# A fused attention and feed-forward layer: residual added by DMA, part of the layer norm and token mix on ACT, new orders of work

## The reference, cut to what matters

```
xn  = layernorm(x)
out = x + attn(xn) + ffn(xn)

attn: q, k, v = silu(short_conv(xn @ Wq)), ...k, ...v ;  beta = sigmoid(xn @ Wb)
      delta   = chunked delta rule(l2norm(q), l2norm(k), v, beta), chunks of 32, a state S carried along L
      ms      = (three depthwise convolutions of v with 3, 15, 31 taps) @ kernel_mix_w @ channel_mixer_w
      hdn     = gelu([xn, mean|ms|, mean|delta|, mean|v|] @ fusion_w1 + b1)
      w       = softmax((hdn @ fusion_w2 + b2) per head over 3)
      o       = rmsnorm(w0 * ms + w1 * delta + w2 * v) * o_norm_w ;  result o @ Wo
ffn:  xp      = xn shifted by one token
      xr      = mu_r * xn + (1 - mu_r) * xp ;  xk = mu_k * xn + (1 - mu_k) * xp
      result  = sigmoid(xr @ W_r.T) * (relu(xk @ W_k.T)^2 @ W_v.T)
```

## Time and profile before

| | |
|---|---|
| median of 3 runs | 3716.8 us (3714.63 to 3717.57) |
| the profiled execution | 3716.15 us |
| its span, first to last instruction | 3714.3 us |
| PE busy | 3491.5 us, 94% |
| DVE busy | 3536.7 us, 95% |
| ACT busy | 2503.4 us, 67% |
| POOL busy | 384.2 us, 10% |
| DMA | 68.08 MB, mean 18 GB/s |

### The profile page before, as it was taken

One profiled execution on the slowest core, in us unless ns is written; L12 is line 12 of the kernel. 1 busy time (PEld: TensorE's weight loads), 2 busy tenths in 40 slices (PEclk: granted clock), 3 DMA queues, 4 the chain that ended last, 5 costly groups with the idle time before them and its releaser, 6 DMA issues. The chain is left out here.

```text
span 3714.3 us, 96880 instructions
## 1 busy us (share of the span) xinstructions
PE 3491.5 (94%) x37184; PEld 2575.8 (69%) x37184; DVE 3536.7 (95%) x8815; ACT 2503.4 (67%) x8246; POOL 384.2 (10%) x369
## 2 busy tenths in 40 slices
PE   7899999999999999999999999999999999999987
PEld 5667777667766677776677666777766776767764
DVE  7999999999999999999999999999999999999994
ACT  4566777667776667776677766677766677666774
POOL 0010110010110101100101101111001111011110
PEclk8999999999999999999999999999999999999998
DMA  4000000000000000000000000000000000000000
GB/s 154 1 19 19 19 2 19 18 19 19 19 2 18 19 19 19 5 16 18 19 19 19 2 18 19 19 19 8 12 18 19 19 19 2 18 19 19 13 7 6
DMA packets 37542, 68.08 MB, mean 18 GB/s; under 512 B 7276, under 2 KB 7788, under 8 KB 37080
## 3 DMA queue, kind: packets, MB, share of 16 engines
q1 hardware_dynamic: 37080, 61.88, 5.3%
HBM read 45.09 MB, written 16.78 MB: 17 GB/s over the span
## 5 line engine op out<-in xcount | busy, mean ns | idle before, releaser
L1426 DVE SCALAR_TENSOR_TENSOR my<-vT,mw,my 128x256 f32<-128x256 f32 x5888 | 2466.1, 482 | 12.4 <-issue 0.2
L631 PE MATMUL dense<-xsh,w 128*128 128x256 f32 x2048 | 483.0, 382 | 0.0
L631 PEld LDWEIGHTS dense<-xsh,w 128*128 128x128 f32 x2048 | 369.5, 190 | 61.3 <-issue 0.3
L384 POOL TENSOR_TENSOR xb<-xb,th 128x512 f32<-128x512 f32 x64 | 92.4, 1443 | 1807.5 <-DVE th L1410 1807.5
L425 PE MATMUL front<-xsh,wv 128*128 128x256 f32 x1024 | 248.9, 398 | 1.8 <-ACT xsh L776 0.8
L609 PE MATMUL dense<-cm,ym 128*128 128x512 f32 x512 | 228.2, 599 | 14.8 <-ACT ym L1014 14.8
L664 PE MATMUL dense<-wo,ms 128*128 128x512 f32 x512 | 240.0, 612 | 2.0 <-ACT ms L1110 1.4
L600 PE MATMUL small<-my,km 128*128 128x256 f32 x768 | 200.1, 397 | 44.1 <-DVE my L1426 34.2
L954 ACT ACTIVATE Bm<-cell,g 128x128 f32<-128x128 f32 x256 | 69.9, 382 | 253.8 <-PE cell L547 253.8
L572 PE MATMUL dense<-xk,wfk 128*128 128x256 f32 x1024 | 239.9, 388 | 0.0
L425 PE MATMUL front<-xsh,wk 128*128 128x256 f32 x1024 | 238.3, 385 | 0.0
(11 more groups left out here) (174 smaller groups left out, 6733.4 us busy)
## 6 DMA issues: line engine op xcount, KB each, us to landing
xa<-in_x SPq DMA_DIRECT2D x32, 512.0 KB, 4.6
xb<-in_x SPq DMA_DIRECT2D x32, 512.0 KB, 4.1
out<-xb SPq DMA_DIRECT2D x32, 512.0 KB, 3.1
w<-in_w SPq DMA_DIRECT2D x1, 2048.0 KB, 16.9
wv<-in_wv SPq DMA_DIRECT2D x1, 1024.0 KB, 7.0
wk<-in_wk SPq DMA_DIRECT2D x1, 1024.0 KB, 8.1
wq<-in_wq SPq DMA_DIRECT2D x1, 1024.0 KB, 8.6
wfk<-in_wfkT SPq DMA_DIRECT2D x1, 1024.0 KB, 7.2
```

The lines of the kernel that those rows point to most:

```text
L384: e.tensor_tensor(xb[s % 2][:, b, :], xb[s % 2][:, b, :], th[:, :], ALU.add).then_inc(residual.sem, 1)
L631: e.matmul(by_batch(o), w1[:, k, hs(2 * pair + c)], xsh[s % 2][:, k, :, 1:1 + P], start=(k == 0), stop=False)
L1426: i = e.scalar_tensor_tensor(o, vT[s % 2][:, c, :, off:off + P], mw[:, col:col + 1], o, ALU.mult, ALU.add)
```

## The change

- SP no longer loads `xb`. It copies `x` to `out` inside HBM (`copy_x`), one step at a time. POOL's `add_residual` is gone; `gate_value` on DVE now works in `xb` itself, `add_attention` adds onto it, and POOL issues the store as a DMA with `accum_op=add` onto `out` (`add_out`), which waits for the copy and for `add_attention`. `tanh_gate` writes to `xb`, and waits for the store of two steps ago. The tile `th` is gone.
- The layer norm's sums move from DVE to ACT: `sum_x` (two copies of 128x512 with an accumulated sum), one tiny `negate_mean` on DVE, `square_x` (two squares of 128x512 with bias and an accumulated sum, their output written to `xsh` as scratch). `bn_stats` and `bn_aggr` are gone.
- The token mix is written as `mu * xn` on ACT (`mix_half`, eight copies of 128x256 with a scale) and `+ (1 - mu) * xp` on DVE (eight multiply-adds, in place). The difference of 128x1024 is gone.
- All four tables of order are rewritten. `half_X`, `kernel_mix(2)`, `key_state(0)` and `project(k, 4)` move across the boundary of a pass or behind other work, `query_key(0)` comes before `turn_x`, and DVE's taps are spread anew. Silu's six calls stand together, and so do gelu's four.

PE's new pass in full, in calls: half_X(c), kernel_mix(c,2), key_state(c,0), ffn_out(c,1), solve(c,0), solve(c,1), outputs(c,0), outputs(c,1), project(k,4), state(c,0), state(c,1), kernel_mix(c,3), channel_mix(c,0), channel_mix(c,1), project(k,5), turn_features(c), hidden(c,0), hidden(c,1), turn_tokens(k,0), hidden(c,2), turn_tokens(k,1), hidden(c,3), logits(c,0), beta_and_q_norm(k), logits(c,1), gram(k,0), turn_logits(c), turn_beta(k), kernel_mix(k,0), gram(k,1), query_key(k,0), kernel_mix(k,1), turn_x(f,0), turn_x(f,1), inverse_W(k,0), project(f,0), inverse_W(k,1), turn_tokens(k,2), query_key(k,1), inverse_Z(k,1), inverse_W(k,2), project(f,1), inverse_Z(k,2), turn_o(c,0), inverse_W(k,3), project(f,2), attend(c,0), turn_o(c,1), inverse_Z(k,3), attend(c,1), inverse_W(k,4), ffn_key(k,0), turn_tokens(k,3), inverse_Z(k,4), project(f,3), inverse_W(k,5), ffn_key(k,1), inverse_Z(k,5), ffn_out(k,0), half_W(k), key_state(k,1).

The diff, cut to its core (the tables of order go on as their first lines do):

```diff
-        bst, mv = sb("bst", P, NB, 6), sb("mv", P, NB, 2)
+        xsum, xneg, xsq = sb("xsum", P, NB), sb("xneg", P, NB), sb("xsq", P, NB)
...
-            def load_residual(s):
+            def copy_x(s):
+
                 if s >= 2:
-                    e.wait_ge(stored, (s - 1) * 16)
-                e.dma_start(xb[s % 2][:, :, :], x[:, s * P:(s + 1) * P, :].rearrange("b p d -> p b d")).then_inc(xb_in[s % 2], 16)
-
-            def store(s):
-                e.wait_ge(*xb_done.upto(s))
-                e.dma_start(out[:, s * P:(s + 1) * P, :].rearrange("b p d -> p b d"), xb[s % 2][:, :, :]).then_inc(stored, 16)
+                    e.wait_ge(stored[s % 2], s // 2 * 16)
+                e.dma_start(out[:, s * P:(s + 1) * P, :], x[:, s * P:(s + 1) * P, :]).then_inc(x_copied[s % 2], 16)
...
             def deviation(s):
-                e.wait_ge(*x_mean.upto(s))
-                e.tensor_scalar(vare[:, :], mv[:, :, 1], 1.0, 1e-5, ALU.mult, ALU.add).then_inc(x_var.sem, 1)
+                e.wait_ge(*x_sq.upto(s))
+                e.tensor_scalar(vare[:, :], xsq[:, :], 1.0 / D, 1e-5, ALU.mult, ALU.add).then_inc(x_var.sem, 1)
...
-            def add_residual(s, b):
-                e.wait_ge(*gated.upto(s, b))
-                e.wait_ge(xb_in[s % 2], s // 2 * 16 + 16)
-                e.tensor_tensor(xb[s % 2][:, b, :], xb[s % 2][:, b, :], th[:, :], ALU.add).then_inc(residual.sem, 1)
+            def add_out(s):
+                e.wait_ge(x_copied[s % 2], s // 2 * 16 + 16)
+                e.wait_ge(*xb_done.upto(s))
+                e.dma_start(out[:, s * P:(s + 1) * P, :].rearrange("b p d -> p b d"), xb[s % 2][:, :, :],
+                            accum_op=ALU.add).then_inc(stored[s % 2], 16)

             for i in range(NS + 2):
                 f, k, c = i < NS, 1 <= i <= NS, i >= 2
-                if c:
-                    add_residual(i - 2, 0)
-                    add_residual(i - 2, 1)
                 if f:
                     deviation(i)
                 if c:
                     invert_o(i - 2, 0)
                 if k:
                     norms_q(i - 1)
+                if c:
+                    invert_o(i - 2, 1)
+                    add_out(i - 2)
+                if k:
                     norms_k(i - 1)
-                if c:
-                    invert_o(i - 2, 1)

...
-                    project(i - 1, 4)
-                if c:
+                if c:
+                    half_X(i - 2)
+                    kernel_mix(i - 2, 2)
+                    key_state(i - 2, 0)
+                    ffn_out(i - 2, 1)
                     solve(i - 2, 0)
                     solve(i - 2, 1)
...
+            def sum_x(s):
+                e.wait_ge(xa_in, s * 16 + 16)
+                if s:
+                    e.wait_ge(*x_neg.upto(s - 1))
+                for b in range(NB):
+                    i = e.activation(xa[:, b, :], xa[:, b, :], ACT.Copy, accum_out=xsum[:, b:b + 1])
+                i.then_inc(x_sum.sem, 1)
+
+            def square_x(s):
+                e.wait_ge(*x_neg.upto(s))
+                if s:
+                    e.wait_ge(*x_var.upto(s - 1))
+                if s >= 2:
+                    e.wait_ge(*hid_mm.upto(s - 2))
+                    e.wait_ge(*mixed_in.upto(s - 2))
+                    e.wait_ge(*bq_mm.upto(s - 2))
+                for b in range(NB):
+                    i = e.activation(xsh[s % 2][:, :, b, 1:1 + P], xa[:, b, :].rearrange("p (c t) -> p c t", c=CB), ACT.Square,
+                                     bias=xneg[:, b:b + 1], accum_out=xsq[:, b:b + 1])
+                i.then_inc(x_sq.sem, 1)

...
+            def mix_half(s):
+                if s == 0:
+                    e.wait_ge(conv_in, 80)
+                e.wait_ge(*xnT_done.upto(s))
+                if s:
+                    e.wait_ge(*key_mm.upto(s - 1))
+                    e.wait_ge(*gate_mm.upto(s - 1))
+                    e.wait_ge(*logits_mm.upto(s - 1))
+                for j, dst in enumerate((xr, xk)):
+                    for c in range(CB):
+                        i = e.activation(by_batch(dst[:, c, :]), xsh[s % 2][:, c, :, 1:1 + P], ACT.Copy, scale=mu[:, j, c:c + 1])
+                i.then_inc(mixed_half.sem, 1)
+
             def relu_key(s, pair):
                 e.wait_ge(*key_mm.upto(s, pair))
-                e.wait_ge(*mixed_in.upto(s))
+                if s:
+                    e.wait_ge(*value_mm.upto(s - 1))
                 e.activation(ka[:, 2 * pair:2 * pair + 2, :], dense[pair][:, :].rearrange("p (c w) -> p c w", c=2),
                              ACT.Relu).then_inc(key_relu.sem, 1)
...
                 e.wait_ge(*gate_mm.upto(s, b))
-                if b:
-                    e.wait_ge(*residual.upto(s, 0))
-                elif s:
-                    e.wait_ge(*residual.upto(s - 1, 1))
-                e.activation(th[:, :], dense[0][:, :], ACT.Tanh, scale=0.5).then_inc(gate_tanh.sem, 1)
+                if s >= 2:
+                    e.wait_ge(stored[s % 2], s // 2 * 16)
+                e.activation(xb[s % 2][:, b, :], dense[0][:, :], ACT.Tanh, scale=0.5).then_inc(gate_tanh.sem, 1)
...
-            def statistics(s):
-                e.wait_ge(xa_in, s * 16 + 16)
-                for b in range(NB):
-                    e.bn_stats(bst[:, b, :], xa[:, b, :]).then_inc(x_stats.sem, 1)
-                if s:
-                    e.wait_ge(*x_normed.upto(s - 1))
-                for b in range(NB):
-                    e.wait_ge(*x_stats.upto(s, b))
-                    e.bn_aggr(mv[:, b, :], bst[:, b, :]).then_inc(x_mean.sem, 1)
+            def negate_mean(s):
+                e.wait_ge(*x_sum.upto(s))
+                if s:
+                    e.wait_ge(*x_sq.upto(s - 1))
+                    e.wait_ge(*x_shift.upto(s - 1))
+                e.tensor_scalar(xneg[:, :], xsum[:, :], -1.0 / D, None, ALU.mult).then_inc(x_neg.sem, 1)

             def mean_shift(s):
                 e.wait_ge(*x_rstd.upto(s))
-                e.scalar_tensor_tensor(nmr[:, :], mv[:, :, 0], -1.0, rstd[:, :], ALU.mult,
-                                       ALU.mult).then_inc(x_shift.sem, 1)
+                if s:
+                    e.wait_ge(*x_normed.upto(s - 1))
+                e.tensor_tensor(nmr[:, :], xneg[:, :], rstd[:, :], ALU.mult).then_inc(x_shift.sem, 1)

...
+            def mix_weights():
+
+                e.wait_ge(conv_in, 80)
+                e.tensor_scalar(rest[:, :, :], mu[:, :, :], -1.0, 1.0, ALU.mult, ALU.add).then_inc(mix_rest, 1)
+
             def mix_in(s):
-                if s == 0:
-                    e.wait_ge(conv_in, 80)
-                e.wait_ge(*xnT_done.upto(s))
-                if s:
+                e.wait_ge(*mixed_half.upto(s))
+                if s == 0:
+                    e.wait_ge(mix_rest, 1)
+                else:
                     e.wait_ge(*shifted.upto(s - 1))
-                    e.wait_ge(*key_mm.upto(s - 1))
-                    e.wait_ge(*gate_mm.upto(s - 1))
-                    e.wait_ge(*logits_mm.upto(s - 1))
-                    e.wait_ge(*value_mm.upto(s - 1))
-                dx, xs = ka[:, :, :].rearrange("p c (b t) -> p c b t", b=NB), xsh[s % 2]
-                e.tensor_tensor(dx, xs[:, :, :, 1:1 + P], xs[:, :, :, 0:P], ALU.subtract).then_inc(x_diff.sem, 1)
-                e.wait_ge(*x_diff.upto(s))
+                xs = xsh[s % 2]
                 for j, dst in enumerate((xr, xk)):
                     for c in range(CB):
-                        e.scalar_tensor_tensor(by_batch(dst[:, c, :]), dx[:, c, :, :], mu[:, j, c:c + 1],
-                                               xs[:, c, :, 0:P], ALU.mult, ALU.add).then_inc(mixed_in.sem, 1)
+                        o = by_batch(dst[:, c, :])
+                        e.scalar_tensor_tensor(o, xs[:, c, :, 0:P], rest[:, j, c:c + 1], o, ALU.mult,
+                                               ALU.add).then_inc(mixed_in.sem, 1)

             def gate_value(s, b):
                 e.wait_ge(*gate_tanh.upto(s, b))
                 e.wait_ge(*value_mm.upto(s, b))
-                e.scalar_tensor_tensor(th[:, :], th[:, :], 1.0, dense[1][:, :], ALU.add,
-                                       ALU.mult).then_inc(gated.sem, 1)
+                t = xb[s % 2][:, b, :]
+                e.scalar_tensor_tensor(t, t, 1.0, dense[1][:, :], ALU.add, ALU.mult).then_inc(gated.sem, 1)

...
+                if i == 1:
+                    mix_weights()
                 if i == 2:
                     prepare_weights()
                 if c:
-                    taps(i - 2, 2, 41, 42)
-                    taps(i - 2, 2, 22, 23)
+                    taps(i - 2, 3, 15, 16)
+                    taps(i - 2, 2, 46, 47)
```

570 lines of the change are left out of this document (270 added, 300 removed).

## The result

The changed kernel took 3695.6 us (median of 5 executions, 3683.95 to 3698.27) beside 3717.6 for the kernel before (5 executions, 3714.63 to 3718.66): a ratio of 0.9933, 95% interval 0.9913 to 0.9952. It is faster by 0.7%, 22 us; the forecast was 3687. The profiled execution took 3697.55 us, with a span of 3695.8 beside 3714.3. The five executions of the changed kernel fall into two groups, 3684 to 3686 us with a mean granted clock of 0.983 and 3696 to 3698 us with 0.979; the profiled one is of the second.

What follows compares the result with a forecast made beforehand. DVE and PE were both taken as full; with DVE relieved, PE's work and waits gave a period of 111.8 us. Thirty periods at -1.3 (-39), clock +5 and ends +4 made -30: 3687 us, range 3612 to 3726.

Steps and rivals of the forecast that it cites:

- the likeliest case: The forecast of 3687 us with 3650 to 3709 around it, given a chance of 0.58.
- DVE's loss of 4.5 us a period: On DVE: sums -1.45, difference -1.2, negate_mean +0.15, POOL's two additions -2.0; work falls from 110.8 to 106.3 us.
- the full exclusion: DVE instructions with two SBUF inputs and POOL's SBUF reads exclude each other entirely; gain on DVE 2.9 us instead of 2.0.
- PE's work of 106.3 us: PE's pure work a period: 113.1 us less 6.8 us of waits with their drains.
- The wait of query_key: PE at query_key(k,0) waits 1.65 us a period for ACT's scale_B(0).
- (b): Rival: ACT is late at copy_logits; with squares 2 us longer, period 113.8 us, time 3747 us; chance 0.13.
- The other waits: PE's remaining waits a period, among them inverse_W, project, attend, outputs, channel_mix and features; all waits together 5.5 us.
- The clock: Seven moments of PE at half clock, each costing 1.7 us instead of 1.05: +5 us in all.
- The ends: Front and back of the run: later first sums, more taps, weigh_v earlier, slower accumulating store; +4 us for both.
- (a): Rival: DVE's whole gain passes, the 2.9 us stretch of PE's waits costing nothing; period 108.9, time 3600 us; chance 0.15.
- (d): Rival: the accumulating DMA holds POOL, delaying norms_k and then scale_v; at 12 us period 114.8, time 3777 us; chance 0.04.
- (c): Rival: gain and ACT's lateness cancel; period 112.8 to 113.0 us, time 3710 to 3723 us; chance 0.10.

Runs made afterwards that it cites:

- e1: The kernel before, with POOL's addition of the residual cut from 512 columns to 8: 3679.7 us, ratio 0.9901.
- e8: The kernel before with the residual's part of the change alone (x copied inside HBM, accumulating DMA from POOL, no addition): 3695.8 us, ratio 0.9943.
- e7: The changed kernel with the layer norm's sums back on DVE (bn_stats and bn_aggr), in the place of negate_mean: 3712.6 us, ratio 0.9982.
- e6: The changed kernel with a plain store by SP in place of copy_x and the accumulating DMA, leaving out x: 3686.5 us, ratio 0.9911.
- e9: The changed kernel with all three moves of work undone, in the new orders, statistics standing where negate_mean was: 3752.0 us, ratio 1.0094.
- e13: The changed kernel with bn_stats and bn_aggr back on DVE, behind short_conv(k,5), and the last block stored plainly: 3683.5 us, ratio 0.9903.
- e5: The changed kernel with scale_B(k,0) moved ahead of first_taps(k,2) on ACT: 3739.2 us, ratio 1.0050.
- e4: The changed kernel with beta's whole chain moved earlier on PE, ACT and DVE: 3783.8 us, ratio 1.0174.
- e12: The changed kernel with only the last block's x loaded into SBUF, added by POOL and stored plainly: 3685.1 us, ratio 0.9921.

## Why the prediction was right, and where its sizes were off

Sign and time came out as forecast: 3687 forecast, 3695.6 measured, within the 3650 to 3709 of the likeliest case. The sum behind it was -30 us; the profiled spans differ by -18.5. That it came as near as this is in part luck: two terms were each off by about as much as the whole result, the undisturbed periods by 20 us one way and the clock by 29 us the other. By its steps:

- **DVE's loss of 4.5 us a period** was right. Its busy time went from 110.11 to 105.75, 4.4 less, and forecast was "about 105". The price of 1.0 us for each addition of POOL, read from three slow taps, is confirmed by e1 and e8 at 1.9 us for two. What was misread is how it comes about. The prediction took the 1.0 of 1.44 us for a milder form of the exclusion, spread over three taps; single instructions show one tap held nearly to the end of POOL's, and no price beyond that because the tap before it was already running. The estimate of 2.9 us for the full exclusion was too high for the same reason.
- **PE's work of 106.3 us** held, or nearly: the period less its listed waits of 3.3 us and a drain of 0.17 us for each of the six and a few unlisted ones is 106.5 to 106.8 us.
- **The wait of query_key** was forecast as 1.65 us for ACT's Bm; it is 1.53, 1.7 with its drain. That the chain through softmax, gains, taps and scale_B gets longer and turns most of DVE's gain into idle time of DVE is what the trace shows: 5.4 us idle ("5 us or more"). That each us lost in the row of ACT's steps is a us of PE (b) leaves out that ACT stands 0.6 us for kernel_mix(k,0) in the middle of that row: e7 frees ACT of the squares and the wait stays at 1.5 us.
- **The other waits** were overestimated. Forecast were 5.5 us in all, drains included, and the period at 111.8. The period is 111.14, which leaves 4.8 us by the same count (3.3 us in the rows of waits, the rest drains and small gaps). With a drain of 0.17 us added to each row, four terms were right: kernel_mix(k,1) for ym, project(f,0), outputs (L549, 0.3 in the row) and channel_mix. The terms that were off: inverse_W(2) and inverse_W(3) at 1.05 and 0.25, where L481 waits 0.5 in all (0.6 with its drain), inverse_W(0) at 0.35, attend at 0.2 and the features at 0.1, where no row shows a wait. The gain is 59 us over thirty periods instead of 39.
- **The clock** was the wrong term. The prediction counted seven moments in the kernel before (the trace has six in the periods that it used), kept them, and charged them 5 us more. In the profiled execution 20 periods hold one, and 40.4 us lie on top of the undisturbed periods instead of 6.5: 34 us of the 59 are given back. Nothing in the earlier trace rows said how often the moments would come; the count of the old kernel was taken over as if it belonged to the program, though the walk itself put a new wait of 1.65 us in one place, and the moments came right behind it.
- **The ends** were forecast at +4. The parts differ (-8.1 ahead, +9.5 and +5.2 behind), the sum is +6.6. The accumulating DMA costs 5 us, inside the bounds of 0 to 6 that were given for it, where the value taken was low. By the Trainium skill's formula for a GpSimd DMA (DMA: Bandwidth & Descriptors, "Anatomy of one DMA") it would have been 3.2 us, an estimate; the measured one is 6.1 from issue to landing, and the measurement decides.
- **The rivals.** (a) wanted PE's waits under 3 us; they are 3.3, so the truth lies between the forecast and (a). (b) wanted 3 us or more at query_key: it has 1.5. (d) wanted ACT's y to wait for POOL's nrm: no such row, and e6 has the same period without the accumulating DMA. For (c) a period of 112.8 us gives 3717 by the prediction's own sum, not 3710.

What the prediction didn't ask is what each part was worth alone. It held the three moves and the orders for one gain. The runs say that the residual's part (e8) has the whole gain by itself, that the new orders with all the old work lose 35 us (e9), some of it by the place of `statistics`, and that the sums can stay on DVE at no cost in time (e13). What the token mix on ACT and the orders are worth singly no run shows.

## What to carry to other kernels

When two engines are both full, a helper engine's instruction that slows one of them (1.44 us of POOL costing DVE 1.0) is the first thing to remove, and it isn't in any row of its own: look for the same instruction at two durations, by its maximum beside its median. A step's cost depends on where it stands: the same 1.3 us of DVE cost 1.33, 1.10 or 0.33 us a period in three places, so before moving work to another engine try a place where one of the engine's waits can take it in. And shortening the largest visible wait by reordering made the period longer three times out of three: in e5 what had stood in front of it was filling a gap, in e4 DVE stood 3.4 us for a step put too early. Read what the reordered step itself waits for. Last, look at where the clock falls and not only how often: here it fell behind PE's waits. That fewer or better spread waits make fewer falls was not shown.

## What the runs showed of the hardware

- An accumulating DMA of 512 KB from SBUF onto HBM, issued by POOL, takes 6.1 us to land (6.2 and 6.3 in e8 and e12) where the plain store takes 3.1, starts 1.0 us after the instruction that it waits for, and is on POOL for 1.26 us; the plain one of e12 starts 0.03 us after. In the steady part it costs nothing (e6: 111.20 beside 111.14).
- One POOL addition of 128x512 (1.44 us) holds one two-input instruction of DVE beside it nearly to its end: 1.49 us instead of 0.48, a loss of 1.0. The Trainium skill (SBUF — State Buffer, "SBUF: two separate sides") has whichever of the two starts first hold the shared ports for its whole instruction; the trace agrees. The 1.0 is less than 1.44 because a tap that had started 0.16 us before POOL ran on undisturbed.
- TensorE's clock fell to 1.2 GHz for 3.41 us in 19 of the first 29 periods although PE was busy 97% of the time before (84.84 of 87.72 us). 19 of the 22 falls came 87.3 to 88.1 us into the period, right behind waits of 1.53 and 0.35 us. Ten periods with the same waits had no fall.
